# The product of attention sums and inverse denominators moved from GpSimd to VectorE

## The chip, the cores and the metric

The kernel runs on one core of a Trainium2 chip. A core has TensorE (PE in the profile, its weight loads PEld), VectorE (DVE), ScalarE (ACT), GpSimd (POOL) and SyncE (SP), which issues most of the DMAs. The metric is the device time of one execution in microseconds, lower is better.

## What is computed

The reference is a chain of four pairs, each a conditioning block and a feed-forward block, on x of 2 x 512 x 128. The change touches the third and the fourth conditioning block. Each is a stack of six transformer layers with 16 heads of 8 dimensions:

```
for i in range(6):
    xn = adaln(x, emb, n1_w[i], n1_b[i])
    q, k, v = split(xn @ qkv_w[i].T)            # rope on q and k
    x = x + attn(q, k, v) @ so_w[i].T           # self-attention, 512 keys
    xn = adaln(x, emb, n2_w[i], n2_b[i])
    q = rope(xn @ cq_w[i].T); k, v from context
    x = x + attn(q, k, v) @ co_w[i].T           # cross-attention, 154 keys
    xn = adaln(x, emb, n3_w[i], n3_b[i])
    x = x + gelu(xn @ f1_w[i].T + f1_b[i]) @ f2_w[i].T + f2_b[i]
```

where attn is softmax(q k^T / sqrt(8)) v. The softmax's division is done last: the sums of exp(score) times v come out of TensorE together with the sums of exp(score), and the first are multiplied by the inverse of the second. That multiplication is what is moved.

## The kernel before

Activations lie transposed: 128 features on the partitions, 512 positions of a batch in the columns, two batches (b = 0, 1). Of a batch's attention, kind a = 0 is self and a = 1 is cross, and the 16 heads are taken in two halves e = 0, 1 of eight heads.

All work of a layer is a list of 371 items with a place each (PLACES, from line 86 on). Every engine walks the same list in the same order and does its part of those items that concern it. An item with a place below 0 or from 371 on belongs to the neighbour layer's stretch, so that the ends of one layer and the beginning of the next are interleaved. Each engine works its own instructions strictly in that order and waits on semaphores in front of them. The order is written out by hand and is the same before and after.

The items around the change, for one (b, a, e):
- score: TensorE's matmuls (L469 self, L476 cross), VectorE's maxima (L807, L809). They share a ring of three PSUM banks, of which an item takes two, so that the matmuls of a score item need the first maximum of the item before it.
- msplit: GpSimd splits the maxima in three parts (L889 to L894), which "turn" on TensorE (L487) transposes; exp: matmuls L498, Exp on ScalarE (L680); pv: TensorE sums exp times v (L524).
- evac: ScalarE copies the sums to SBUF, osb (L699). sel: TensorE spreads the denominators with a selector matrix (L541), ScalarE takes their logarithm (L706). inv: ScalarE makes rinv = exp(-log) (L712), and GpSimd multiplies osb by rinv into att (L899).
- out: TensorE projects att when both halves are there (L553), VectorE adds to h (L818).
- center, var, apply: the layer norm; TensorE L572 and L583, ScalarE L718, L719, L726, L729, VectorE L827, L830. proj: TensorE L597, VectorE rotates (L844, L848). hi and st: the rotated tile is split (ScalarE L739, GpSimd L905 to L910) and stacked by DMAs from SP and ACT (L439), which the score matmuls wait for. f1, f2: the feed-forward part.
- hold (L364): matmuls without use of their own in chosen idle places of TensorE.

The eight inv items of a layer have these places in the list:

```
    ('inv', 0): [[93, 144], [284, 293]],
    ('inv', 1): [[210, 265], [352, 369]],
```

that is (b = 0, self, e = 0) at 93, (b = 0, self, e = 1) at 144, (b = 0, cross) at 284 and 293, (b = 1, self) at 210 and 265, (b = 1, cross) at 352 and 369. VectorE's own items around them are: scores at 89, 94 and 95 around 93; scores at 141, 142, 143, the output projection's sum at 145 and scores from 148 on around 144; scores at 209 and 214 around 210; a score at 261 and the sum of out at 271 around 265; between 284 and 293 nothing, then apply of batch 1's second norm at 294, its projection at 296 and the sum of out at 298; the next layer's projections at 348 and 350 ahead of 352; the sum of out at 370 behind 369.

GpSimd's list held msplit, inv, hi and ktail, VectorE's score, out, apply, proj, gain, biasf and f2. The semaphore den_inv counts ScalarE's L712, att_ready counts the products; att_ready is waited for by out on TensorE and, two products later, by evac and inv on ScalarE, which write the same buffers again.

Of the kernel before, what the change touches and what calls it, by code (L numbers as in the profile page):

```python
# [69 lines left out]
def unit_order():  # L70

    work = []
    for u in range(UNITS2):
        for name, at in UNIT_AT.items():
            if isinstance(at, float):
                work.append((at + UNIT_US * u, (name, u)))
            else:
                work += [(t + UNIT_US * u, (name, u, n)) for n, t in (at.items() if isinstance(at, dict) else enumerate(at))]
    return [(item, 0) for _, item in sorted(work, key=lambda x: x[0])]
# [171 lines left out]
def floor0(count):  # L251
    return max(count, 0) if isinstance(count, int) else count


def build(nc, dram):

    with ExitStack() as ctx:
# [3 lines left out]
        def sem(name):  # L261
            return ctx.enter_context(nc.semaphore(name))
# [32 lines left out]
        def carve(cols, dt=F32):  # L295
            a = arena[:, used[0]:used[0] + cols]
            used[0] += -(-cols // 8) * 8
            assert used[0] <= ARENA, used[0]
            return a if dt == F32 else a.bitcast(dt)
# [8 lines left out]
        ktail = [carve(2 * 4 * 160 // 2, BF16).rearrange("p (e n) -> p e n", e=2) for b in range(B)]  # L308
# [13 lines left out]
        att = carve(B * 2 * S).rearrange("p (b e n) -> p b e n", b=B, e=2)  # L322
        osb = carve(2 * S).rearrange("p (e n) -> p e n", e=2)
        rlog = lg[:, S:2 * S]
        rinv = carve(2 * S).rearrange("p (e n) -> p e n", e=2)
# [22 lines left out]
        pv_mm, pvt_mm, max_split, den_inv, att_ready = (sem(n) for n in ("pv_mm", "pvt_mm", "max_split", "den_inv", "att_ready"))  # L348
# [7 lines left out]
        def cols(a, b, width=S):  # L356
            return a[:, b * width:(b + 1) * width]
# [48 lines left out]
        def s_bank(slot):  # L406
            return bank(slot % RING["s"])
# [4 lines left out]
        def pack(n):  # L412
            return min(3, 8 - 3 * n)
# [7 lines left out]
        def unit_cols(a, b, u):  # L421
            return a[:, unit(b, u), 0:B * CTX if u == 3 else S]
# [369 lines left out]
        def stack_dve_items(ve, z, layer, at_last=None):  # L792
            def bias_of(it):
                base, turn = layer[0] + z.layer_of[it], layer[1]
                if turn is None:
                    return bias_all[:, base * NBIAS:(base + 1) * NBIAS]
                return bias_all[:, base * NBIAS:][:, bass.ds(turn * NBIAS, NBIAS)]

            def score(it):
                _, b, a, g, n = it  # L800
                slot, at = z.use("s", it)
                if n == 0:
                    ve.wait_ge(max_split, floor0(z.ahead("group", it) - 4))
                for r in range(2):
                    ve.wait_ge(s_full, at + r + 1)
                    if a == 0:
                        op = ve.tensor_reduce(nmax[:, g % 2, r, n:n + 1], s_bank(slot + r), AX.X, ALU.max, negate=True)  # L807
                    else:
                        op = ve.tensor_reduce(nmax[:, g % 2, r, 3 * n:3 * n + pack(n)],  # L809
                                              s_bank(slot + r)[:, 0:pack(n) * CTX].rearrange("p (i n) -> p i n", n=CTX),  # L810
                                              AX.X, ALU.max, negate=True)
                    op.then_inc(s_free, 1 + (z.skipped("s", it) if r == 0 else 0))

            def out(it):
                _, b, a = it
                slot, at = z.use("s", it)
                ve.wait_ge(s_full, at + 1)
                ve.tensor_tensor(cols(h, b), s_bank(slot), cols(h, b), ALU.add).then_inc(s_free, 1 + z.skipped("s", it))  # L818

            def apply(it):  # L820
                _, b, k = it
                ve.wait_ge(rstd_ready, z.after("rstd", ("var", b, k), it))
                if k == 3:
                    ve.tensor_tensor(cols(h, b), cols(centered, b), cols(rstd, b), ALU.mult).then_inc(ln_applied, 1)
                    return
                ve.wait_ge(s_free, z.ahead("s", it))
                ve.scalar_tensor_tensor(cols(centered, b), cols(centered, b), gains[:, k, 0, b:b + 1], cols(rstd, b), ALU.mult,  # L827
                                        ALU.mult).then_inc(scaled, 1)
                ve.wait_ge(scaled, z.after("scaled", it))
                ve.tensor_scalar(cols(xn, b), cols(centered, b), gains[:, k, 1, b:b + 1], None, ALU.add).then_inc(ln_applied, 1)  # L830

            def proj(it):
                _, b, u = it
                slot, at = z.use("s", it)
                n = B * CTX if u == 3 else S
                ve.wait_ge(rope_sum, z.ahead("rope", it))
                for i in range(2):
                    ve.wait_ge(s_full, at + i + 1)
                    if u == 3:
                        turn = rope[:, i, 0:CTX].unsqueeze(1).broadcast_to([P, B, CTX])  # L840
                        op = ve.tensor_tensor(turned_q[:, i, 0:n].rearrange("p (b n) -> p b n", b=B),
                                              s_bank(slot + i)[:, 0:n].rearrange("p (b n) -> p b n", b=B), turn, ALU.mult)
                    else:
                        op = ve.tensor_tensor(turned_q[:, i, :], s_bank(slot + i), rope[:, i, :], ALU.mult)  # L844
                    op.then_inc(s_free, 1 + (z.skipped("s", it) if i == 0 else 0))
                ve.wait_ge(s_free, at + 2)
                ve.wait_ge(part_lo, z.ahead("hi", it))
                ve.tensor_tensor(unit_cols(rotated, b, u), turned_q[:, 0, 0:n], turned_q[:, 1, 0:n], ALU.add)\  # L848
                  .then_inc(rope_sum, 1)

            def gain(it):
                k = it[1]
                slot, at = z.use("s", it)
                ve.tensor_copy(bias_n[:, 2 * k:2 * k + 2], bias_of(it)[:, 2 * k:2 * k + 2])\
                  .then_inc(bias_copied, 1)
                ve.wait_ge(bias_copied, z.after("bias", it))
                ve.wait_ge(s_full, at + 1)
                ve.tensor_tensor(gains[:, k], s_bank(slot)[:, 0:4].rearrange("p (w b) -> p w b", w=2),
                                 bias_n[:, 2 * k:2 * k + 2].unsqueeze(2).broadcast_to([P, 2, B]), ALU.add)\
                  .then_inc(s_free, 1 + z.skipped("s", it))  # L860

            def biasf(it):
                ve.tensor_copy(bias_f[:, 0:5], bias_of(it)[:, 6:11])\
                  .then_inc(bias_copied, 1)

            def f2(it):
                b = it[1]
                slot, at = z.use("s", it)
                if at_last is not None:
                    at_last()  # L870
                ve.wait_ge(bias_copied, z.ahead("bias", it))
                ve.wait_ge(s_full, at + 1)
                ve.scalar_tensor_tensor(cols(h, b), s_bank(slot), bias_f[:, 4:5], cols(h, b), ALU.add, ALU.add)\
                  .then_inc(s_free, 1 + z.skipped("s", it))

            does = {"score": score, "out": out, "apply": apply, "proj": proj, "gain": gain, "biasf": biasf, "f2": f2}
            for it, _ in z.order:
                if it[0] in does:
                    does[it[0]](it)

        def stack_pool_items(gp, z):
            def msplit(it):
# [9 lines left out]
                gp.tensor_tensor(mid, now, hi, ALU.subtract).then_inc(max_split, 1)  # L892
                gp.wait_ge(max_split, at + 3)
                gp.tensor_tensor(lo, rest, mid, ALU.subtract).then_inc(max_split, 1)  # L894

            def inv(it):
                _, b, a, e = it
                gp.wait_ge(den_inv, z.after("inv", it))
                gp.tensor_tensor(att[:, b, e, :], osb[:, e, :], rinv[:, e, :], ALU.mult).then_inc(att_ready, 1)  # L899

            def hi(it):
                _, b, u = it
# [9 lines left out]
            def tails(it):  # L912
# [4 lines left out]
                                          zeros[:, 0:1].unsqueeze(2).unsqueeze(3).broadcast_to([P, 2, 4, 32]), ALU.add)  # L917
                op.then_inc(ktail_made, 1)

            does = {"msplit": msplit, "inv": inv, "hi": hi, "ktail": tails}  # L920
            for it, _ in z.order:
                if it[0] in does:
                    does[it[0]](it)
# [1569 lines left out]
        def stack_pool(gp, c):  # L2493
            x_is(c["x"])(gp, 1)
            stack_walk(gp, c, lambda z, l: stack_pool_items(gp, z))
# [20 lines left out]
        for k in range(FIRST, LAST + 1):  # L2516
# [4 lines left out]
            else:  # L2521
                counts[k] = dict(c)
                if k == 2:
                    z = Stretch(unit_order(), dict(c["counted"]))
# [193 lines left out]
```

## Time and profile before

| | |
|---|---|
| time before, median of 3 runs | 3567.42 us (3567.13 to 3568.31) |
| profiled execution, first to last instruction | 3577.0 us |
| granted TensorE clock, mean | 0.938 |
| busy: TensorE, VectorE, ScalarE, GpSimd | 3016.5, 2087.9, 1911.5, 808.3 us |
| products L899 | 96, median 1272 ns |
| layers of the two stacks | 12, some 218 us each |

A row of a timeline gives the start in us from the span's start, the time from the first to the last of its instructions, the engine (a name with q is its queue), line, operation, the tiles out<-in, their shapes and the count; in brackets stands how long the engine was idle before and who ended that. The granted clock is 1.00 at 2.4 GHz and 0.50 at 1.2 GHz.

### The profile page before, as it was taken

The numbers are of one execution on the slowest core, as the hardware profiler recorded it, in microseconds if no ns is written. First come the engines' busy times: TensorE is split into PE (matmuls) and PEld (weight loads), VectorE is DVE, ScalarE is ACT, GpSimd is POOL, SyncE is SP. The second block draws the span as 40 slices with busy tenths as digits, with TensorE's granted clock in tenths as the row PEclk, the third lists the DMA queues.
The fourth block names the chain that finished last, engine by engine and source line by source line (L and its number), as shares of the span: only waits on it lengthen the run. The fifth ranks groups of instructions, "written<-read, shape, count | busy, mean of one in ns | idle before, by whom it ended". The sixth has DMA issues, their size and how long they took to land.

```text
span 3577.0 us, 50916 instructions
## 1 busy us (share of the span) xinstructions
PE 3016.5 (84%) x15735; PEld 1057.7 (30%) x15735; DVE 2087.9 (58%) x3631; ACT 1911.5 (53%) x2693; POOL 808.3 (23%) x1327
## 2 busy tenths in 40 slices
PE   7998999868888788887878856888888787887878
PEld 2463333222222222222222222222222222222226
DVE  4326777447475664846558367558375564746634
ACT  5433333337466574665647534647466474665642
POOL 0003455512212222221212102212212222212211
PEclk9999999879999998999999987989999999999999
DMA  1100000001110101101011001011110111101020
GB/s 42 54 17 8 1 1 1 11 26 36 32 37 27 46 23 32 46 24 46 26 30 40 21 11 42 25 32 40 33 36 27 41 28 32 41 22 51 19 96 34
DMA packets 125571, 110.74 MB, mean 31 GB/s; under 512 B 49982, under 2 KB 116076, under 8 KB 125292
## 3 DMA queue, kind: packets, MB, share of 16 engines
q1 hardware_dynamic: 114924, 97.80, 9.3%
q10 hardware_dynamic: 10368, 9.44, 0.9%
q8 instruction: 148, 2.42, 0.3%
q14 instruction: 131, 1.07, 0.1%
HBM read 41.96 MB, written 0.52 MB: 12 GB/s over the span
## 4 chain that ended last, share of the span: by engine, by line
PE 61%; DVE 16%; issue 7%; ACT 6%; POOL 5%; SPq 2%; ACTq 2%; DMA 0%; DVEq 0%; POOLq 0%
PE ps L524 10%; DVE arena L807 7%; PE ps L469 6%; PE ps L498 4%; PE ps L655 4%; PE ps L597 3%; PE ps L640 3%; ACT arena L680 3%; PE ps L583 2%; PE ps L553 2%; PE ps L1501 2%; PE ps L541 2%; PE ps L532 2%; PE ps L572 2%; PE ps L1489 2%
## 5 line engine op out<-in xcount | busy, mean ns | idle before, releaser
L680 ACT ACTIVATE arena<-ps 128x1024 f32<-128x1024 f32 x960 | 936.8, 1024 | 349.2 <-PE ps L498 345.4
L807 DVE TENSOR_REDUCE arena<-ps 128x1 f32<-128x512 f32 x1536 | 967.3, 685 | 217.6 <-PE ps L469 193.4
L524 PE MATMUL ps<-arena 128*32 128x512 f32 x3840 | 513.6, 609 | 20.5 <-ACT arena L680 18.0
L469 PE MATMUL ps<-arena 49*128 49x512 bf16 x1536 | 318.9, 412 | 249.0 <-DVE arena L807 202.0
L498 PE MATMUL ps<-arena 52*128 52x512 bf16 x1920 | 346.7, 387 | 27.9 <-ACT arena L680 24.7
L809 DVE TENSOR_REDUCE arena<-ps 128x3 f32<-128x462 f32 (+1 forms) x576 | 303.7, 580 | 84.8 <-PE ps L476 80.9
L889 POOL TENSOR_TENSOR arena<-arena,zeros 128x16 bf16<-128x16 f32 x192 | 42.6, 222 | 1052.3 <-DVE arena L807 631.2
L469 PEld LDWEIGHTS ps<-arena 49*128 49x128 bf16 x1536 | 75.3, 94 | 593.5 <-DVE arena L807 493.9
L899 POOL TENSOR_TENSOR arena<-arena 128x512 f32<-128x512 f32 x96 | 122.2, 1272 | 455.3 <-ACT arena L712 455.3
L905 POOL TENSOR_TENSOR arena<-arena 128x512 bf16<-128x512 f32 (+1 forms) x84 | 92.6, 1102 | 546.5 <-ACT arena L739 546.5
L818 DVE TENSOR_TENSOR h<-ps,h 128x512 f32<-128x512 f32 x48 | 33.2, 692 | 295.8 <-PE ps L553 295.8
L827 DVE SCALAR_TENSOR_TENSOR tmp<-tmp,arena,rstd 128x512 f32<-128x512 f32 x72 | 54.1, 752 | 252.2 <-ACT rstd L729 249.9
L1561 ACT ACTIVATE arena<-ps 128x1024 f32<-128x1024 f32 x96 | 98.2, 1023 | 167.1 <-DVE ps L1648 130.1
L364 PE MATMUL ps<-consts 128*128 128x512 f32 x336 | 163.1, 611 | 23.7 <-DVE arena L2085 23.7
L498 PEld LDWEIGHTS ps<-arena 52*128 52x128 bf16 x1920 | 86.9, 94 | 313.1 <-ACT arena L680 195.1
L1731 POOL TENSOR_TENSOR arena<-arena 128x1024 f32<-128x1024 f32 x64 | 150.5, 2352 | 36.1 <-ACT arena L1561 34.8
L597 PE MATMUL ps<-xn,w 128*128 128x512 f32 x288 | 145.4, 630 | 8.0 <-DVE xn L830 7.4
L718 ACT ACTIVATE sq<-ps 128x512 f32<-128x512 f32 x76 | 45.2, 595 | 196.0 <-PE ps L572 195.5
L541 PE MATMUL ps<-arena,selector 128*128 128x512 f32 x192 | 106.7, 638 | 39.1 <-ACT arena L699 33.4
L844 DVE TENSOR_TENSOR arena<-ps,rope 128x512 f32<-128x512 f32 x144 | 99.6, 692 | 67.9 <-PE ps L597 65.0
L476 PE MATMUL ps<-arena 49*128 49x154 bf16 x1536 | 101.5, 231 | 43.6 <-DVE arena L809 38.2
L1648 DVE TENSOR_TENSOR ps<-ps,arena 128x1024 f32<-128x1024 f32 x96 | 116.5, 1228 | 36.3 <-PE ps L1489 36.3
(383 smaller groups left out, 4393.4 us busy)
## 6 DMA issues: line engine op xcount, KB each, us to landing
arena<-arena SPq DMA_DIRECT2D x720, 64.0 KB
arena<-we_dram SPq DMA_DIRECT2D x24, 578.5 KB, 7.8
arena<-arena ACTq DMA_DIRECT2D x144, 64.0 KB
w<-weights_dram SPq DMA_DIRECT2D x26, 320.0 KB, 3.1
w<-weights_dram SPq DMA_DIRECT2D x13, 512.0 KB, 3.7
arena<-arena SPq DMA_DIRECT2D x384, 6.0 KB
arena<-arena SPq DMA_DIRECT2D x288, 19.2 KB
w<-weights_dram SPq DMA_DIRECT2D x39, 128.0 KB, 2.1
```

Source lines behind the costliest of these rows:

```text
L364: pe.matmul(dst, center, consts[:, :], start=True, stop=True)
L469: pe.matmul(s_bank(slot + r), qst[b][rows, idx, P * qt:P * (qt + 1)], kst[b][rows, idx, :], start=True, stop=True).then_inc(s_full, 1 + (z ...
L498: mm = pe.matmul(e_bank(slot)[:, S * r:S * (r + 1)], (kst, kstc)[a][b][rows, 2 * g + p, P * kt:P * (kt + 1)], qst[b][rows, 2 * g + p, :], ...
L524: mm = pe.matmul(bank(7)[32 * j:32 * j + 32, :], v, prob[:, slot, j, :], start=(g % 2 == 0 and kt == 0), stop=(a == 0 and g % 2 == 1 and k ...
L541: pe.matmul(e_bank(slot)[:, 0:S], selector2[:, :], osb[:, e, :], start=True, stop=True)\
L597: pe.matmul(s_bank(slot + i)[:, 0:B * CTX if u == 3 else S], w[:, base + P * i:base + P * (i + 1)], src, start=True, stop=True).then_inc(s ...
L655: mm = pe.matmul(s_bank(slot), w[:, W_F2 + P * t:W_F2 + P * (t + 1)], hid[:, t, :], start=(t == 0), stop=(t == FT - 1))
L680: act.activation(prob[:, chunk_no(b, a, g, kt) % NPROB, 2 * p:2 * p + 2, :], e_bank(slot).rearrange("p (j n) -> p j n", j=2), ACT.Exp, sca ...
L807: op = ve.tensor_reduce(nmax[:, g % 2, r, n:n + 1], s_bank(slot + r), AX.X, ALU.max, negate=True)
L809: op = ve.tensor_reduce(nmax[:, g % 2, r, 3 * n:3 * n + pack(n)], s_bank(slot + r)[:, 0:pack(n) * CTX].rearrange("p (i n) -> p i n", n=CTX ...
L899: gp.tensor_tensor(att[:, b, e, :], osb[:, e, :], rinv[:, e, :], ALU.mult).then_inc(att_ready, 1)
L1731: gp.tensor_tensor(sum2[0:n, :, :], sum2[0:n, :, :], prob2[0:n, j], ALU.add).then_inc(s2["summed"], 1)
```

## The change

The function inv moves from GpSimd's functions to VectorE's, with its place in the list, its operands and its two semaphores:

```diff
@@ stack_dve_items
+            def inv(it):
+                _, b, a, e = it
+                ve.wait_ge(den_inv, z.after("inv", it))
+                ve.tensor_tensor(att[:, b, e, :], osb[:, e, :], rinv[:, e, :], ALU.mult).then_inc(att_ready, 1)
+
...
-            does = {"score": score, "out": out, "apply": apply, "proj": proj, "gain": gain, "biasf": biasf, "f2": f2}
+            does = {"score": score, "out": out, "inv": inv, "apply": apply, "proj": proj, "gain": gain, "biasf": biasf, "f2": f2}
@@ stack_pool_items
-            def inv(it):
-                _, b, a, e = it
-                gp.wait_ge(den_inv, z.after("inv", it))
-                gp.tensor_tensor(att[:, b, e, :], osb[:, e, :], rinv[:, e, :], ALU.mult).then_inc(att_ready, 1)
-
...
-            does = {"msplit": msplit, "inv": inv, "hi": hi, "ktail": tails}
+            does = {"msplit": msplit, "hi": hi, "ktail": tails}
```

## Rows read from the trace of the kernel before

**Rows 1.** The page: busy us (share of the span) and instructions.
```profile
PE 3016.5 (84%) x15735; PEld 1057.7 (30%) x15735; DVE 2087.9 (58%) x3631; ACT 1911.5 (53%) x2693; POOL 808.3 (23%) x1327
```

**Rows 2.** Line L899: durations, ns min/median/max; who waited for it, us, times.
```profile
L899 POOL TENSOR_TENSOR arena<-arena x96: 1262/1272/1287, 814.9 to 3443.7; 128x512 f32<-128x512 f32 x96
...
  PE ps L553: 12.3, 12
```

**Rows 3.** Groups of VectorE, 800 to 3450 us: count, busy us, mean ns, idle before.
```profile
L824 DVE TENSOR_TENSOR h<-tmp,rstd 128x512 f32<-128x512 f32 x2 | 1.4, 694 | 5.8 <-ACT rstd L729 5.8
```

**Rows 4.** Timeline around the product at place 93.
```profile
1029.72 0.63 ACT L712 ACTIVATE arena<-lg 128x512 f32<-128x512 f32 x1
...
1030.43 1.28 POOL L899 TENSOR_TENSOR arena<-arena 128x512 f32<-128x512 f32 x1 [2.63 <-ACT arena L712]
...
1029.33 2.48 DVE L807 TENSOR_REDUCE arena<-ps 128x1 f32<-128x512 f32 x4 [0.71 <-PE ps L469]
...
1028.91 0.39 PE L469 MATMUL ps<-arena 49*128 49x512 bf16 x2
1030.08 0.39 PE L469 MATMUL ps<-arena 49*128 49x512 bf16 x2 [0.78 <-DVE arena L807]
...
1030.73 2.85 ACT L680 ACTIVATE arena<-ps 128x1024 f32<-128x1024 f32 x3 [0.38 <-PE ps L498]
```

**Rows 5.** Timeline around place 144.
```profile
1051.44 0.63 ACT L712 ACTIVATE arena<-lg 128x512 f32<-128x512 f32 x1
...
1051.05 3.73 DVE L807 TENSOR_REDUCE arena<-ps 128x1 f32<-128x512 f32 x6 [0.55 <-PE ps L469]
...
1053.59 3.46 PE L553 MATMUL ps<-arena,w 128*128 128x512 f32 x4
...
1057.41 1.02 ACT L680 ACTIVATE arena<-ps 128x1024 f32<-128x1024 f32 x1 [5.34 <-PE ps L498]
```

**Rows 6.** Timeline around place 210.
```profile
1086.82 0.63 ACT L712 ACTIVATE arena<-lg 128x512 f32<-128x512 f32 x1
...
1088.06 1.18 DVE L809 TENSOR_REDUCE arena<-ps 128x3 f32<-128x462 f32 x2
1089.53 0.64 DVE L809 TENSOR_REDUCE arena<-ps 128x3 f32<-128x462 f32 x1 [0.29 <-PE ps L476]
```

**Rows 7.** VectorE's idle time behind the products at places 265 and 284.
```profile
1111.55 0.69 DVE L818 TENSOR_TENSOR h<-ps,h 128x512 f32<-128x512 f32 x1 [5.98 <-PE ps L553]
...
1122.90 0.75 DVE L827 SCALAR_TENSOR_TENSOR tmp<-tmp,arena,rstd 128x512 f32<-128x512 f32 x1 [10.66 <-ACT rstd L729]
```

**Rows 8.** Timeline around place 293 (L827 stands in the group before).
```profile
1123.69 0.49 DVE L830 TENSOR_SCALAR xn<-tmp,arena 128x512 f32<-128x512 f32 x1
...
1124.05 1.12 PE L541 MATMUL ps<-arena,selector 128*128 128x512 f32 x2 [0.72 <-ACT arena L699]
1125.01 1.88 PE L597 MATMUL ps<-xn,w 128*128 128x512 f32 x4
...
1125.92 0.63 ACT L712 ACTIVATE arena<-lg 128x512 f32<-128x512 f32 x1
```

**Rows 9.** Timeline around place 352.
```profile
1170.81 1.68 DVE L848 TENSOR_TENSOR arena<-arena 128x512 f32<-128x512 f32 x1
```

**Rows 10.** Timeline around place 369, and the start of another layer's scores.
```profile
1182.23 1.98 PE L553 MATMUL ps<-arena,w 128*128 128x512 f32 x4 [1.05 <-POOL arena L899]
...
1184.25 0.69 DVE L818 TENSOR_TENSOR h<-ps,h 128x512 f32<-128x512 f32 x1 [11.76 <-PE ps L553]
...
1186.30 0.61 PE L469 MATMUL ps<-arena 49*128 49x512 bf16 x2 [2.08 <-issue]
...
968.50 0.39 PE L469 MATMUL ps<-arena 49*128 49x512 bf16 x2 [0.88 <-DVE h L818]
```

**Rows 11.** Stretches: length; busy us of PE, PEld, DVE, ACT, POOL; granted clock; DMA.
```profile
1186.30:1189.70 3.40, 2.08 (x5) 0.70 (x6) 2.12 (x4) 0.00 (x0) 0.00 (x0) 0.50 0.03 7
...
1030.40:1248.30 217.90, 183.83 (x1034) 57.77 (x1032) 132.69 (x223) 129.93 (x177) 47.65 (x96) 0.94 0.12 34
```

## Prediction

> **What bounds the kernel now.** I read the page first, then the list of groups, then the timeline around each of the eight products of one layer, one engine at a time, then the granted clock. The reader should see in the page that TensorE leads: it is busy 84% of the span, VectorE 58%, ScalarE 53% and GpSimd 23% [rows 1]. GpSimd's 96 products last 1.27 us each, and TensorE was seen waiting for one of them only 12 times, 12.3 us together: once in each of 12 layers [rows 2]. So the product as such is worth little. What matters is its place in VectorE's order, because an engine takes its instructions one behind the other: while VectorE waits for ScalarE's Exp (L712), the work behind it waits too, and TensorE, whose order is fixed as well, waits for that. The eight places of a layer repeat in all 12 layers with offsets that differ by some 0.1 us, so I work with the layer that begins at about 1030 us and multiply.
>
> **The parts.** Removed: 96 times 1.27 us on GpSimd, which is idle before most of them. Added: 96 products on VectorE. VectorE's sum of two 128x512 f32 tiles in SBUF, L824, takes 0.69 us [rows 3]; the same form (L848) takes 1.68 us beside a GpSimd tensor operation [rows 9]. I take 0.69, since at seven of the eight places no long GpSimd operation runs; 1.68 is the other end and matters at the seventh alone. From the end of the Exp to the start of the product I take 0.08 us, as on GpSimd: 1030.43 behind 1030.35 [rows 4]. Each place, with what is queued behind the wait:
>
> First (place 93). The Exp ends at 1029.72 + 0.63 = 1030.35. VectorE now does the four reduces of two score items from 1029.33 to 1031.81; in the new order the product stands before them, so they begin at 1030.35 + 0.08 + 0.69 = 1031.12 in place of 1029.33: 1.79 us later. The second score item's matmul (1030.08, seen waiting for L807) needs the first reduce, so TensorE stops as long, and ScalarE, which was already waiting for TensorE at 1030.73, does too [rows 4]. All three fronts move: +1.79. If it were absorbed later it would be 0.
>
> Second (place 144). Its Exp ends at 1052.07, early, but VectorE has six reduces before the product, until 1051.05 + 3.73 = 1054.78. The product then ends at about 1055.49. The output projection L553 started at 1053.59 and would start at about 1055.5: +1.9. Nothing covers it: ScalarE is idle 5.34 us there already [rows 5]. Here no wait is added; the product only comes later than on an idle GpSimd.
>
> Third (place 210). The Exp (to 1087.45) is over before the reduces are, so the product is put in at 1088.14 without a wait, and the cross-attention reduces move 0.69 back. VectorE idles 0.29 us before the next [rows 6], so 0.4 us is left: +0.4, ends 0 and 0.69.
>
> Fourth and fifth (265, 284). VectorE is idle 5.98 us ahead of L818 and 10.66 us ahead of L827 [rows 7], and the output projection behind the fourth did not wait for the product: 0. Without that cover each would cost 0.69.
>
> Sixth (place 293). This is the large one. VectorE's order is now: apply the layer norm (L827 at 1122.90, L830 to 1124.18), then the query projection's rotation. In the new order the product of ScalarE's last Exp stands before L827. That Exp ends at 1125.92 + 0.63 = 1126.55, so the product runs to 1127.32 and L827, L830 end at about 1128.63, in place of 1124.18. L597 needs their output; it started at 1125.01, behind L541, and will start at about 1128.67: +3.66 [rows 8]. Behind it stand the rotation, the split, the stacking DMAs, the scores that wait for those, and on the other branch the output projection, its norm and the first feed-forward layer: all of it follows L597 in TensorE's order. The wait is thus 3.65 us of VectorE at a place where it worked at once before. Across the layers: 3.6 to 3.7.
>
> Seventh (place 352). The product comes behind L848 and beside a GpSimd split; even at 1.68 us it is hidden, since VectorE is idle 11.76 us ahead of L818 [rows 9, 10]. GpSimd's next split starts about 1.2 us earlier, but the stacking DMAs are issued back to back from SP without a wait for it: 0.
>
> Eighth (place 369). VectorE is idle, the product ends 1.27 - 0.69 = 0.58 us earlier and L553, which waited 1.05 us for L899, gains nearly all of it, 0.56. At six of the ten borders between layers the next scores start some 1.3 us behind L818 (1186.30 against 1184.94), held by the stacking DMAs, and give it back; at four they follow L818 at once, as at 968.50 [rows 10]. With the two last layers of the stacks six gains are kept: -3.4 us in all, ends 0 and -6.7.
>
> Sum without the clock: 12 x (1.79 + 1.9 + 0.4 + 3.66) = 93.0, minus 3.4: +89.6 us.
>
> **The clock.** The sixth place gives TensorE an idle stretch from the end of L541 at 1125.17 to 1128.67, 3.5 us. The nearest row: after an idle 2.08 us the clock was 0.50 of full speed, which is 1.2 GHz, from 1186.30 on, while idle stretches of 1.05 us as before L553 left it at 2.4 GHz [rows 10, 11]. L553's four matmuls take 3.46 us in such a low stretch and 1.98 at full clock [rows 5, 10], and L597's four are the same work: +1.5 us. Ends: 0 and 1.5 at the sixth place; 0 and 1.5 at the first, where TensorE now idles 2.5 us (1029.30 to 1031.87); at the second, L553 already runs at the low clock, and moving it by 1.9 us can give back 0.9 or cost 0.8 more. I take 1.5 at the sixth and nothing at the others: 12 x 1.5 = +18.
>
> The Trainium skill ("TensorE: Matmul & The Clock Gate", What's actually happening) says the low clock is the default and that it is TensorE's activity that lifts it; by it the stall would be paid twice, once as time and once in slower matmuls, and the rows of the stretch after 1186.30 agree. By that page the sum is 107.6, without it 89.6.
>
> The Trainium skill ("SBUF — State Buffer", SBUF: two separate sides) says that a VectorE operation with two SBUF inputs and a GpSimd operation that reads SBUF take one port by an exclusive lock. The 1.68 us of L848 agrees; by it the seventh product would be long, in a stretch where VectorE has nothing else to do.
>
> The sum goes on the profiled execution, 3577.0 us, which is 9.6 us (0.3%) above the median of 3567.42; the places are the same in both, so I add 107.6 to the median: 3675 us.
>
> **The rivals.**
> A. The same stalls, but the clock holds: 89.6 us, 3657 us. For it: TensorE is dense before the sixth place. Against it: 2.08 us of idle were enough for the row at 1186.30.
> B. The clock falls at the first and second place as well: 12 x (1.5 + 0.8) = 27.6 more, 3703 us. For it: the stretch before the second place is thin already, and L553 there ran at the low clock (3.46 us) [rows 5].
> C. The stalls of the first three places are absorbed by later slack, as all three engines idle somewhere in a layer, and the sixth alone counts: 12 x (3.66 + 1.5) - 3.4 = 58.5, 3626 us. Against it: TensorE's order is fixed, and nothing that it waits for later runs free of it.
> D. The other side, not slower: VectorE's hold is covered by matmuls already queued, and what remains is the earlier start of the output projection at the eighth place, 12 x 0.56 = 6.7 us, 3561 us. It decides at the sixth place: it needs 3.6 us of TensorE work between L541 and L597 that does not use L830's output. The rows have L597 0.96 us behind L541's start, with nothing between [rows 8]. The same time would come out if the product did not wait in VectorE's order. The Trainium skill ("Perfetto Trace Analysis", Optimizing Scalar/DVE Operations) warns that moving work between VectorE and GpSimd might not help, because of their common port; by it the move changes little, which is D's direction, and the trace agrees only beside a GpSimd operation, as at L848's 1.68 us.
>
> **How the numbers follow.** Forecast 0.62, A 0.15, B 0.11, C 0.08, D 0.04. The range goes from C's time to a little beyond B's, 3628 to 3710 us. What a measurement can tell from no change is about 0.2%, 7 us; D straddles this: faster 0.02, same 0.02, slower 0.96.
>
> **What would show it.** In the profile after: L597 of the sixth place starts some 3.6 us later relative to L541, with the granted clock at 0.50 behind it; L807 at the first place starts right behind the product, 0.77 us after the Exp; L553 at the second waits for a VectorE product, some 1.9 us more; L553's wait for the product at the eighth shrinks by half a microsecond; a layer grows from 217.9 us [rows 11] to about 227. VectorE's new group has 96 products of 0.69 us, ten of them longer. I am wrong if the layer grows by less than 5 us, if L597 is not held, or if the growth sits in another place.

## The result and the profile after

The changed kernel takes 3684.51 us (median of 4 runs, 3680.56 to 3694.9) against 3567.28 us (median of 4) of the kernel before. The ratio is 1.033, 95% interval 1.031 to 1.0349: slower by 117 us, where 3675 us was forecast. In a later set (e11 below) the same two stood at 1.0282 (1.0224 to 1.034).

The profiled execution's span grew from 3577.0 to 3681.3 us. The page after has less GpSimd and more VectorE work, and TensorE is busy 38 us longer with the same 15735 matmuls, so some of them ran slower:

```profile
PE 3054.6 (83%) x15735; PEld 1067.0 (29%) x15735; DVE 2155.6 (59%) x3727; ACT 1910.5 (52%) x2693; POOL 695.2 (19%) x1231
```

Against [rows 1], VectorE gained 67.7 us. The span grew by more than that, although VectorE is idle 41% of it. The product is now line 823; its own rows give the durations (ns, min/median/max), then who waited for it (us, times):

```profile
L823 DVE TENSOR_TENSOR arena<-arena x96: 676/692/1640, 815.0 to 3552.7; 128x512 f32<-128x512 f32 x96
...
  PE ps L553: 29.4, 23
```

[rows 2] had 1272 ns and 12 waits of 12.3 us together. The operation is faster and is waited for longer. Where the time went is read place by place, in the layer that begins at 1037 us, in timelines like those above. Line numbers from 823 on have moved in the new file: L832 and L835 are the layer norm's L827 and L830.

**First place**, against [rows 4]. The Exp ends at 1037.32. VectorE stands idle, makes the product, and only then the four reduces; the second score item's matmul waits 2.43 us:

```profile
1036.69 0.63 ACT L712 ACTIVATE arena<-lg 128x512 f32<-128x512 f32 x1
...
1037.35 0.69 DVE L823 TENSOR_TENSOR arena<-arena 128x512 f32<-128x512 f32 x1 [1.75 <-ACT arena L712]
1037.96 2.47 DVE L807 TENSOR_REDUCE arena<-ps 128x1 f32<-128x512 f32 x4
...
1035.88 0.39 PE L469 MATMUL ps<-arena 49*128 49x512 bf16 x2
1038.70 0.39 PE L469 MATMUL ps<-arena 49*128 49x512 bf16 x2 [2.43 <-DVE arena L807]
1038.93 0.60 PE L498 MATMUL ps<-arena 52*128 52x512 bf16 x4
1039.46 1.77 PE L524 MATMUL ps<-arena 128*32 128x512 f32 x8
```

Measured from the Exp's end, that matmul comes at +1.38 us; before it came at 1030.08 - 1030.35 = -0.27. The stall is 1.65 us. L524's eight matmuls behind it take 1.77 us. In the kernel before the same eight took 1.07:

```profile
1030.84 1.07 PE L524 MATMUL ps<-arena 128*32 128x512 f32 x8
```

**Second place**, against [rows 5]. The product follows six reduces, and the output projection waits 2.09 us for it:

```profile
1061.31 0.63 ACT L712 ACTIVATE arena<-lg 128x512 f32<-128x512 f32 x1
...
1060.92 3.68 DVE L807 TENSOR_REDUCE arena<-ps 128x1 f32<-128x512 f32 x6 [0.56 <-PE ps L469]
1064.52 0.68 DVE L823 TENSOR_TENSOR arena<-arena 128x512 f32<-128x512 f32 x1
...
1065.34 3.75 PE L553 MATMUL ps<-arena,w 128*128 128x512 f32 x4 [2.09 <-DVE arena L823]
```

The Exp ended at 1061.31 + 0.63 = 1061.94, so L553 is at +3.40 against 1053.59 - 1052.07 = +1.52: a stall of 1.88 us. The four matmuls take 3.75 us, at the low clock as before (3.46).

**Third place**, against [rows 6]: the product takes 0.68 us at once behind the reduces. GpSimd's first split, beside it, takes 0.60 us in place of the 0.22 us of its followers:

```profile
1100.47 0.68 DVE L823 TENSOR_TENSOR arena<-arena 128x512 f32<-128x512 f32 x1
1101.07 2.28 DVE L809 TENSOR_REDUCE arena<-ps 128x3 f32<-128x462 f32 x4
...
1100.63 0.60 POOL L894 TENSOR_TENSOR arena<-arena,zeros 128x16 bf16<-128x16 f32 x1 [10.44 <-DVE arena L807]
1101.31 0.22 POOL L896 TENSOR_TENSOR arena<-arena 128x16 f32<-128x16 f32 x1
```

**Sixth place**, against [rows 8]: VectorE waits for the Exp (to 1139.17) ahead of the layer norm, whose last input (ScalarE's L729) was complete at 1135.49, and TensorE has nothing to do between L541 and L597:

```profile
1139.20 0.69 DVE L823 TENSOR_TENSOR arena<-arena 128x512 f32<-128x512 f32 x1 [6.88 <-ACT arena L712]
1139.81 0.74 DVE L832 SCALAR_TENSOR_TENSOR tmp<-tmp,arena,rstd 128x512 f32<-128x512 f32 x1
1140.59 0.49 DVE L835 TENSOR_SCALAR xn<-tmp,arena 128x512 f32<-128x512 f32 x1
...
1136.67 1.12 PE L541 MATMUL ps<-arena,selector 128*128 128x512 f32 x2 [0.72 <-ACT arena L699]
1141.21 2.94 PE L597 MATMUL ps<-xn,w 128*128 128x512 f32 x4 [3.41 <-DVE xn L835]
1143.95 3.52 PE L364 MATMUL ps<-consts 128*128 128x512 f32 x6
1147.30 1.88 PE L553 MATMUL ps<-arena,w 128*128 128x512 f32 x4
```

L597 stands 4.54 us behind L541's start, before 0.96: a stall of 3.58 us. L597 takes 2.94 us, before 1.88. The stretches, with the columns of [rows 11], show the granted clock: 1.00 in a stretch without one matmul, then 0.63 and 0.87. The second place's L553 lies at 0.50, and the whole layer, 227.60 us in place of 217.90, at 0.92 in place of 0.94:

```profile
1037.40:1265.00 227.60, 188.51 (x1030) 59.12 (x1030) 138.33 (x231) 129.93 (x177) 38.31 (x87) 0.92 0.12 33
1137.80:1141.20 3.40, 0.00 (x0) 0.00 (x0) 1.84 (x3) 1.23 (x2) 0.00 (x0) 1.00 0.00 0
1141.20:1144.60 3.40, 3.39 (x5) 1.50 (x6) 1.10 (x2) 0.00 (x0) 0.00 (x0) 0.63 0.00 0
1144.60:1148.00 3.40, 3.40 (x8) 1.48 (x7) 0.97 (x2) 0.63 (x1) 1.52 (x2) 0.87 0.04 10
1065.30:1068.70 3.40, 3.36 (x4) 1.18 (x4) 0.00 (x0) 0.00 (x0) 0.00 (x0) 0.50 0.14 32
```

**Seventh and eighth place**, against [rows 9, 10]. Beside GpSimd's L910 the product at the seventh place takes 1.64 us, with nothing waiting behind it on VectorE. At the eighth, L553 waits 0.44 us in place of 1.05, and the next layer's scores still wait for the stacking DMAs:

```profile
1189.76 1.64 DVE L823 TENSOR_TENSOR arena<-arena 128x512 f32<-128x512 f32 x1
...
1189.43 1.42 POOL L910 TENSOR_TENSOR arena<-arena 128x512 bf16<-128x512 f32 x1
...
1198.95 1.98 PE L553 MATMUL ps<-arena,w 128*128 128x512 f32 x4 [0.44 <-DVE arena L823]
1203.47 0.60 PE L469 MATMUL ps<-arena 49*128 49x512 bf16 x2 [2.54 <-DMA arena<-arena]
```

To add up all 12 layers I took the ends of the 96 L712 in both traces and subtracted them pair by pair. The difference is how far the changed kernel has fallen behind at that point. The table sums how much it grows from one place to the next, in us:

| stretch, 12 layers | forecast | measured |
|---|---|---|
| first to second place | 21.5 | 25.1 |
| second to third | 22.8 | 29.7 |
| third to fourth | 4.8 | 2.3 |
| fourth to sixth | 0 | 0.0 |
| sixth to seventh | 43.9 + 18 | 59.4 |
| seventh over eighth to the next first | -3.4 | -7.6 |
| all | 107.6 | 108.9 |

Outside these stretches the changed kernel's profiled execution was 4.6 us shorter, which makes the span's 104.3. The last stretch is no firm measure: in the traces of e2, e3 and e5 below, which leave the seventh and eighth products on GpSimd, it moves by -13.0, +0.8 and -11.0 us.

### The profile page after: what moved, and what is told of

Same layout as the page of the kernel before. It is cut to its first block, busy times and chain, and to the rows that moved or that the text cites. A ratio compares the mean times of both kernels' runs of the same rounds, so it can differ in the third digit from the quotient of the medians.

```text
span 3681.3 us, 50916 instructions
## 1 busy us (share of the span) xinstructions
PE 3054.6 (83%) x15735; PEld 1067.0 (29%) x15735; DVE 2155.6 (59%) x3727; ACT 1910.5 (52%) x2693; POOL 695.2 (19%) x1231
## 4 chain that ended last, share of the span: by engine, by line
PE 63%; DVE 17%; ACT 8%; issue 7%; POOL 2%; ACTq 2%; SPq 1%; DVEq 0%; DMA 0%; POOLq 0%
PE ps L524 10%; DVE arena L807 7%; PE ps L469 6%; PE ps L597 4%; PE ps L498 4%; PE ps L655 4%; ACT arena L680 3%; PE ps L640 3%; PE ps L553 3%; PE ps L541 3%; PE ps L583 2%; DVE arena L809 2%; PE ps L1501 2%; PE ps L572 2%; PE ps L532 2%
## 5 line engine op out<-in xcount | busy, mean ns | idle before, releaser
L524 PE MATMUL ps<-arena 128*32 128x512 f32 x3840 | 515.2, 611 | 20.5 <-ACT arena L680 18.0
L823 DVE TENSOR_TENSOR arena<-arena 128x512 f32<-128x512 f32 x96 | 75.6, 787 | 315.1 <-ACT arena L712 315.1
L597 PE MATMUL ps<-xn,w 128*128 128x512 f32 x288 | 164.4, 701 | 48.3 <-DVE xn L835 47.7
L541 PE MATMUL ps<-arena,selector 128*128 128x512 f32 x192 | 107.7, 643 | 39.3 <-ACT arena L699 33.6
L553 PE MATMUL ps<-arena,w 128*128 128x512 f32 x192 | 115.2, 731 | 29.4 <-DVE arena L823 29.4
L655 PE MATMUL ps<-arena,w 128*128 128x512 f32 x192 | 132.2, 853 | 3.8 <-DVE arena L809 2.8
```

The lines of the kernel that those rows point to most:

```text
L524: mm = pe.matmul(bank(7)[32 * j:32 * j + 32, :], v, prob[:, slot, j, :], start=(g % 2 == 0 and kt == 0), stop=(a == 0 and g % 2 == 1 and k ...
L541: pe.matmul(e_bank(slot)[:, 0:S], selector2[:, :], osb[:, e, :], start=True, stop=True)\
L553: mm = pe.matmul(s_bank(slot), w[:, base + P * e:base + P * (e + 1)], att[:, b, e, :], start=(e == 0), stop=(e == 1))
L597: pe.matmul(s_bank(slot + i)[:, 0:B * CTX if u == 3 else S], w[:, base + P * i:base + P * (i + 1)], src, start=True, stop=True).then_inc(s ...
L655: mm = pe.matmul(s_bank(slot), w[:, W_F2 + P * t:W_F2 + P * (t + 1)], hid[:, t, :], start=(t == 0), stop=(t == FT - 1))
```

## The experiments

Theory H: what costs is VectorE's place in the order, where the product or the wait for it holds other work, and the clock that falls in the gaps. Rival W: what costs is VectorE's added work (the 96 L823, 75.6 us together), wherever it stands. Ratios are to the kernel before on the same chip; e1 to e8 ran on one chip, e9 to e11 on a second, e12 on a third. In some kernels both engines make products; the product then also waits for att_ready of those made by the other engine, which are long done. Where the text speaks of us at the low clock, it is the time within the named stretch of all 12 layers in which the granted clock was 0.50.

**e1, e2: one place taken back, and one place alone.**

```diff
+        ON_DVE = [(0, 1, 1)]              # e2; in e1 the other seven
...
+                if it[1:] in ON_DVE:      # VectorE's inv; GpSimd's has "not in"
+                    make_inv(ve, z, it)
```

> The changed kernel with one of the eight products of a layer, the sixth (place 293), back on GpSimd. Theory H (what costs is that VectorE stands before the product and holds the work behind it): the profile after has L597 3.58 us later here, plus some 1.3 us of slower matmuls, 12 layers: about 60 us below the changed kernel's 3684, so 3625 us. Rival W (what costs is VectorE's added work, 76 us in all, wherever it stands): an eighth of the 117 us goes, so about 3670 us.

> The kernel before with only the sixth product (place 293) moved to VectorE. H: 12 x (3.6 + 1.3) = 59 above 3567, so 3626 us. W: an eighth of 117 us, so 3582 us. If the two kernels of this pair do not add up to the whole 117 us, the places act on each other through the clock.

Measured: e1 3631.74 us, ratio 1.0185 (1.0151 to 1.0219); e2 3618.61 us, ratio 1.0126 (1.0094 to 1.0158). Added alone, this one product of eight costs 45 us, not the 15 of W. Taken back, it gives 52 us against the 1.033 of the first set, and 35 against the 1.0282 of the second. In e2's profile L597 follows L541's start (1124.23) by 4.63 us, waits 3.50 and takes 3.78 us, twice its 1.88: stall and low clock from this place alone.

```profile
1128.86 3.78 PE L597 MATMUL ps<-xn,w 128*128 128x512 f32 x4 [3.50 <-DVE xn L845]
```

**e3: the wait without the product.** All products on GpSimd; at place 293 VectorE only waits.

```diff
+                elif it[1:] in [(0, 1, 1)]:
+                    ve.wait_ge(den_inv, z.after("inv", it))
```

> The kernel before with all products on GpSimd; VectorE only waits for the sixth place's Exp (den_inv) in front of its own next instruction, without making the product. H: the wait alone costs what the move of this product costs, less the product's 0.69 us: 12 x (2.9 + 1.3) = 50, so 3617 us. W: no work is added to VectorE, so 3567 us, no change.

Measured: 3639.43 us, ratio 1.0197 (1.0169 to 1.0225). W is out as the whole cause: VectorE has no added work here and the kernel is 70 us slower. But the wait alone costs more than wait and product together (e2, 21 us less), which I had not expected. The timeline (VectorE, then GpSimd) shows a part of the reason: both engines are released by the same Exp, GpSimd's product starts, and the layer norm's first step (L827 of the kernel before, here L844) beside it takes 1.70 us in place of 0.75:

```profile
1125.58 1.70 DVE L844 SCALAR_TENSOR_TENSOR tmp<-tmp,arena,rstd 128x512 f32<-128x512 f32 x1 [14.50 <-ACT arena L712]
1127.31 0.49 DVE L847 TENSOR_SCALAR xn<-tmp,arena 128x512 f32<-128x512 f32 x1
...
1125.47 1.26 POOL L801 TENSOR_TENSOR arena<-arena 128x512 f32<-128x512 f32 x1 [6.30 <-ACT arena L712]
```

xn is complete 2.41 us behind the Exp's end (1127.80 - 1125.39); in e2, with the product made by VectorE in between, 2.00 us (1128.73 - 1126.73). Over the layers this is 12 x 0.41 = 5 us of the 21. All twelve L844 of this place are long, 1.34 to 1.85 us. In the two traces the stretch from the sixth to the seventh place grows by 66.4 and 56.7 us, 9.7 apart, with 102 and 82 us at the low clock. The rest of the 21 us is not explained.

**e4: the same engine, another place.** All eight on VectorE; the sixth behind the rotation of item 296.

```diff
+            LATE = {('proj', 1, 2): ('inv', 0, 1, 1)}
             for it, _ in z.order:
-                if it[0] in does:
+                if it[0] in does and it not in LATE.values():
                     does[it[0]](it)
+                if it in LATE:
+                    inv(LATE[it])
```

> The changed kernel, all eight products on VectorE, but VectorE makes the sixth behind the query projection's rotation (place 296) in place of ahead of the layer norm (294); the output projection that needs it is at 298. H: the same as with this product on GpSimd, about 3625 us, since only the place counts. W: same work on VectorE, so no change from 3684 us.

Measured: 3625.82 us, ratio 1.0157 (1.0128 to 1.0185), the time of e1 within the intervals: no difference shows between the two engines as makers of this product. What counts is what stands behind it. L832 starts when its own input is there, and L597 follows L541 by 0.96 us as in [rows 8]:

```profile
1135.54 0.75 DVE L832 SCALAR_TENSOR_TENSOR tmp<-tmp,arena,rstd 128x512 f32<-128x512 f32 x1 [3.20 <-ACT rstd L729]
...
1136.69 1.12 PE L541 MATMUL ps<-arena,selector 128*128 128x512 f32 x2 [0.72 <-ACT arena L699]
1137.65 1.88 PE L597 MATMUL ps<-xn,w 128*128 128x512 f32 x4
```

**e5, e6, e7: the other places.** The kernel before with ON_DVE = (0, 0, 0), with (0, 0, 1), and with the four quiet ones.

> The kernel before with only the first product (place 93) on VectorE. The move ahead of the four reduces holds all three engines 1.65 to 1.8 us in each layer: 12 x 1.7 = 20, and some slower matmuls where the clock falls, so 3567 + 20 to 27, about 3590 us. If later slack took the stall back (rival C of the prediction) it would be 3567.

> The kernel before with only the second product (place 144) on VectorE: the product stands behind six reduces and the output projection waits 1.9 us longer. 12 x 1.9 = 23, with the clock 23 to 32: about 3594 us. Rival C: 3567 us.

> The kernel before with the four products on VectorE at whose places it is idle (265, 284, 352, 369). The three first cost nothing, the eighth gives 0.56 us in about six of twelve layers: 3567 - 3.4 = 3564 us, at most 6.7 us below. If VectorE's added 33 us of work cost anything, it would be above 3567.

Measured: e5 3600.09 us, 1.0082 (1.0065 to 1.0099), or 29 us; e6 3612.77 us, 1.0118 (1.0101 to 1.0135), or 42 us; e7 3577.75 us, 1.0013 (1.0001 to 1.0026), or 5 us. Rival C of the prediction, that these stalls are taken back, is out. The single effects, 45 (e2) + 29 + 42 + 5, make 121 us without the third place, which has no run of its own; the whole move costs 117 and 101 in its two sets. So the places roughly add up. e5 costs 29 where its stall is 12 x 1.65 = 20, and e6 costs 42 where its stall is 12 x 1.9 = 23. In their traces the stretch behind the moved product grows by 27.9 and 36.7 us. e7 does not gain the forecast 3.4 us. In its trace L553 waits 0.43 us for the product, so the gain at the eighth place is there. At this border, the one of [rows 10], the next scores then wait 2.70 us in place of 2.08 and give it back, as the prediction has it for six borders of ten:

```profile
1174.90 1.98 PE L553 MATMUL ps<-arena,w 128*128 128x512 f32 x4 [0.43 <-DVE arena L801]
1179.58 0.39 PE L469 MATMUL ps<-arena 49*128 49x512 bf16 x2 [2.70 <-issue]
```

Its ratio is a little above 1, with an interval that nearly touches it; what those 5 us are I can't say. Between the first product and the last its trace is as long as the one of before within 0.3 us: the last stretch of the table is 6.4 us shorter, and the one from the sixth to the seventh place 5.2 us longer, with 61 us at the low clock in place of 51.

**e8: matmuls in the sixth place's gap.** The changed kernel, with three hold matmuls while TensorE waits; their results are not used.

```diff
+                    if it == ("proj", 1, 2):
+                        pe.wait_ge(s_free, z.room("s", it, 1))
+                        hold(pe, s_bank(slot), 3)
                     pe.wait_ge(ln_applied, z.after("ln", ...))
```

> The changed kernel with three hold matmuls (L364's kind, 0.86 us each at full clock) put into TensorE's 3.4 us of idle time at the sixth place, ahead of its wait for L835. The stall in time stays, the idle does not. If the clock's fall behind this gap costs 1 to 1.5 us a layer, 3684 goes down by 12 to 18, to about 3669 us. If the stall alone is what costs, 3684 stays.

Measured: 3668.82 us, 1.0271 (1.0254 to 1.0288) against 1.033 (1.031 to 1.0349) of the changed kernel. Against the changed kernel's second set, on another chip, 1.0282 (1.0224 to 1.034), it can't be told apart, so the gain in the kernel's time is not shown. Its trace shows what it does to this place. L597 (here L600) is as late as ever, 4.46 us behind L541, but takes 1.98 us, and the hold group behind it 2.74 us in place of 3.52:

```profile
1133.22 1.12 PE L541 MATMUL ps<-arena,selector 128*128 128x512 f32 x2 [0.72 <-ACT arena L702]
1134.18 2.74 PE L364 MATMUL ps<-consts 128*128 128x512 f32 x6
1137.68 1.98 PE L600 MATMUL ps<-xn,w 128*128 128x512 f32 x4 [0.76 <-DVE xn L838]
1139.50 2.74 PE L364 MATMUL ps<-consts 128*128 128x512 f32 x6
```

In the same sum over twelve layers the stretch from the sixth to the seventh place grows by 44.5 us in place of 59.4 (59.0 in e11's trace); 12 x 3.6 = 43 is the stall alone. So 15 us of this place are the clock's. Part of them is lost elsewhere: the stretch from the first to the second place, which the edit does not touch, grows by 36.1 us in place of 25.1, with 48 us at the low clock in place of 20.

**e9: three products moved in VectorE's order; e10: holds at the second place; e11: the changed kernel again.**

```diff
+            LATE = {('proj', 1, 2): ('inv', 0, 1, 1), ('score', 0, 0, 3, 7): ('inv', 0, 0, 0),
+                    ('score', 1, 0, 1, 3): ('inv', 0, 0, 1)}      # e9
...
-        FILL = {("out", 0, 1): 3,
+        FILL = {("out", 0, 0): 2, ("out", 0, 1): 3,               # e10, on e6's kernel
```

> The changed kernel, all eight products on VectorE, three of them at another point of VectorE's own order: the first behind the four reduces (behind place 95), the second ahead of the last score item (behind 142), the sixth behind the rotation (behind 296). Theory H: the first and sixth stalls go, of the second some 0.7 of 1.9 us stays, the third's 0.2 stays: 12 x 0.9 = 11 us and a few us of clock above the kernel before, a ratio of about 1.004. W (the added work costs): the ratio stays at 1.033.

> The kernel with only the second product on VectorE, and two hold matmuls (0.86 us each) in TensorE's idle time ahead of its output projection. That kernel cost 42 us where the stall alone is 12 x 1.9 = 23. If the other 19 us are the clock's, most of them go: a ratio of about 1.007 in place of 1.0118. If the surplus has another cause it stays at 1.0118.

> The changed kernel once more, on the chip of the runs of this call, as their common measure: a ratio of 1.033 as before.

Measured: e9 3583.26 us, 1.0021 (0.9995 to 1.0047); e10 3583.32 us, 1.0018 (0.9996 to 1.0039); e11 3679.65 us, 1.0282 (1.0224 to 1.034). e9 makes all 96 products on VectorE and can't be told from the kernel before, while e11, the unchanged order on the same chip, is 2.8% slower: W falls here once more. In e9's trace, the fastest of its ten executions, the stretches behind the first, second and sixth place grow by -0.4, 12.3 and 0.0 us in place of 25.1, 29.7 and 59.4. Its first product stands in the gap that VectorE has behind the reduces:

```profile
1020.23 2.48 DVE L807 TENSOR_REDUCE arena<-ps 128x1 f32<-128x512 f32 x4 [0.71 <-PE ps L469]
1022.63 0.68 DVE L823 TENSOR_TENSOR arena<-arena 128x512 f32<-128x512 f32 x1
```

e10 takes back some 36 of e6's 42 us (by ratios from two chips; the profiled executions are 28 us apart), more than the 19 that I gave to the clock. In its trace L553 takes 2.80 us; in e6's 3.75:

```profile
1048.06 2.81 PE L364 MATMUL ps<-consts 128*128 128x512 f32 x4 [0.21 <-DVE arena L818]
1050.65 2.80 PE L553 MATMUL ps<-arena,w 128*128 128x512 f32 x4
```

The stretch behind the second place shrinks by 13 us against e6's. Another 14 us come from the stretch behind the sixth, which neither edit touches and where less time was granted at the low clock (17 us over 12 layers in place of 48; 35 to 61 in the other traces that leave the sixth product on GpSimd or move it behind the rotation). That the clock elsewhere shifts with it is what this one trace shows; why just there stays open.

**e12: the same hold in the kernel before.** FILL gets ("out", 0, 0): 1, nothing else.

> The kernel before with one hold matmul ahead of the output projection at place 145 (behind the second product), and nothing else changed. The hold costs up to 0.86 us a layer, since the projection hardly waited; if it lifts the low clock in which the projection's four matmuls take 3.46 in place of 1.98 us, a layer gains 1.5 - 0.86 = 0.6 us: 12 x 0.6 = 7 us, ratio 0.998. If the low stretch begins ahead of the hold anyway, 12 x 0.9 = 10 us are lost, or twice that at the low clock: ratio 1.003 to 1.006.

Measured: 3580.55 us, 1.0022 (1.0005 to 1.0039): a small loss, on the side of the second branch but below its 1.003. In the layer read the hold did not lift the clock: it took 2.08 us, and L553 behind it 3.62 us against 3.46 before:

```profile
1052.22 2.08 PE L364 MATMUL ps<-consts 128*128 128x512 f32 x2
1054.09 3.62 PE L553 MATMUL ps<-arena,w 128*128 128x512 f32 x4
```

In its trace the stretch behind the second place grows by 8.8 us and the one behind the sixth shrinks by 7.3. No version that I ran beats the kernel before.

## Why the prediction was right, and where it was off

- The mechanism, that the places and not the work cost, was right: e3 and e9 show it from both sides, e4 for the largest place.
- Sixth place: stall 3.66 forecast, 3.58 measured; clock 1.5 forecast, (59.4 - 43)/12 = 1.4 in the profile, and e8's trace shows that it is the clock. The sign named for it, 0.50 behind L597, came as 0.63 in the layer read. The rule of the Trainium skill ("TensorE: Matmul & The Clock Gate", What's actually happening), that activity lifts the clock, thus agrees with the runs; rival A fell.
- First place: stall 1.79 forecast, 1.65 measured. I counted the product's 0.69 us in full, but the reduce behind it starts 0.61 us after it (1037.96 - 1037.35), and the product 0.03 us behind the Exp, not 0.08.
- Second place: stall 1.9 forecast, 1.88 measured.
- The term that was too small is the clock at these two, set to nothing: the stretches grew by 5.3 and 7.1 us beyond their stalls in the changed kernel. e10 shows it for the second; for the first only L524's 1.77 us in place of 1.07 speaks for it, no run tests it. Rival B put 27.6 us there, so in the whole move the truth lay between. Moved alone (e5, e6) the two grew by 8.1 and 14.1 us beyond their stalls in the traces.
- Third place: 4.8 forecast, 2.3 measured; the product was hidden in part.
- Eighth place: L553's wait shrank by 0.61 us as forecast. The stretch around it gave 7.6 us in place of 3.4 in the profile, but it moves as far where the eighth product is not touched (-13.0 us in e2's trace), and e7 gives no gain in time. So this term is not confirmed.
- Rival D fell with the result and with e2, rival C with e5 and e6.
- That the profile's 108.9 us in the layers hit 107.6 is luck: the missing clock (12.4 us) is offset by smaller stalls, the cheaper third place, the sixth's 59.4 in place of 61.9, and 4.2 us of the last stretch, which is noise as far as is known. The medians moved by 117, the second set's by 2.8% or 101; the two sets bracket the forecast. The stated range begins at 3628, 2 us above the time of rival C that it was to start from.

## What to carry to other kernels

Before an operation goes to an engine that is idle much of the time (VectorE here 42%), write down when its input arrives at its place in that engine's order and what stands behind it: a faster operation in front of work that is ready costs the whole wait, and a few items further on it may cost nothing. Price a new gap on TensorE twice, as time and as slower matmuls behind it. When one of two engines waits for an event that also releases the other, ask whether the two released operations use SBUF side by side.

## What the runs showed of the hardware that I had not expected

- VectorE's f32 operations with both tensors in SBUF and GpSimd's tensor operations held each other up in the rows read. It was visible for L848 before (1.68 us). In e3 the layer norm's L844 takes 1.70 us in place of 0.75, and in the changed kernel GpSimd's 0.22 us split takes 0.60. VectorE's L844 of the kernel before, with one input in PSUM, takes 0.69 us in all 144 cases, though 38 of them overlap a GpSimd operation by more than 0.3 us. The exclusive lock of the Trainium skill ("SBUF — State Buffer", SBUF: two separate sides) agrees with these rows.
- Two hold matmuls in a gap that a stall had made took a ratio from 1.0118 (e6) to 1.0018 (e10); one hold where there was no such gap took it from 1 to 1.0022 (e12).
- The clock of one place can change with an edit at another: with e10's edit at the second place the low-clock time behind the sixth was 17 us in place of e6's 48, and with e8's at the sixth that behind the first was 48 in place of 20. Each is one execution.
